# Second division of a window moved from unit 9 to unit 12, another choice of units whose second exponential goes to SBUF, and one store one place later in the queue

## The chip, the cores and the metric

The kernel runs on one core of a Trainium2 chip. The metric is the device time of one execution in microseconds (us). The kernel before was run three times: median 2611.41 us, from 2608.67 to 2623.45. Another execution was taken with the profiler; its rows are the ones shown below.

## The reference, cut to what matters

A cross-attention (64 pairs of batch and head, 1024 queries each from `x`; 1024 keys from `x` and 77 from `ctx_1024`, padded to 9 tiles of 128; head width 64), then a shared expert and a top-2 mixture of 8 experts. The part that the change touches is the softmax and its normalisation:

```python
sim = jnp.einsum('bhid,bhjd->bhij', qn, kn)
attn = jax.nn.softmax(sim, axis=-1)
out = jnp.einsum('bhij,bhjd->bhid', attn, v)
```

The kernel computes the unnormalised sum over the keys with the exponentials, gets the sum of the exponentials as a 65th row of the same product (V has a column of ones), and divides afterwards.

## The kernel before, in words

**Windows and units.** The attention runs in 32 windows of two heads (`WINDOWS`), preceded by two opening ones that only prepare. One window has 18 units (`UNITS`, 9 tiles of keys for each of two blocks g of 512 queries; both heads are in a unit, one in each half of the columns). So "the sums h = 0" (`o_sb[0]`, named o_first) are the first block of 512 queries of both heads, ready after unit 8, and h = 1 (`o_second`) those of the second block, ready after unit 17.

**One unit d** takes these steps. TensorE computes scores into one of two PSUM buffers, `ps_s[:, d % 2]` (line 975, 128 keys by 1024 columns). ScalarE takes the exponential twice: once rounded to fp32r as `pr_hi` (line 831), once in fp32 (line 832), either back into the same PSUM buffer or, for the units in `SPARED` (line 83, through `full_of`), into an SBUF buffer `pr[:, d % 2]`. VectorE subtracts the two to get the low part `pr_lo` (line 721); I call it the subtraction of unit d. TensorE multiplies V with both parts (line 1011, in two halves of the keys; line 997 for the first two units) into `ps_o`, two and three units later (`first`, `second`).

**What SPARED decides.** TensorE may write the scores of unit d + 2 into the buffer of unit d when nobody reads it any more: for a spared unit when the exponentials are done (`s_exp`), for the others when VectorE's subtraction is done (`s_lo`):

```python
wait(pe, s_exp if (d - 2) % UNITS in SPARED else s_lo, w.n(UNITS, d - 1))
```

The units after 17 are units 0, 1, ... of the next window. ScalarE waits before a spared unit for the subtraction two units before, because of the buffer `pr`.

**The sums.** After the ninth tile of keys VectorE copies the 65 x 1024 sums from PSUM to `o_sb[h]` (`output`, line 652): h = 0 ahead of the subtraction of unit 10, h = 1 ahead of that of unit 1 of the next window. `ps_o` is single, so TensorE's first product of the next block (unit 9, issued in `first` of unit 11; unit 0, in unit 2) waits for that copy through `s_o`.

**The division** is a round trip through DRAM. SyncE's queue stores the row of sums of exponentials and loads it back spread over 128 partitions (`spread`), VectorE inverts it (`invert`, line 681, after units 5 and 13), SyncE stores it and loads it broadcast to 64 partitions into `rec` (`broadcast`), and VectorE multiplies (`divide`, line 686): in the next window h = 0 after unit 7, h = 1 after unit 9. `rec` is one buffer for both. The result is stored by SyncE (`store`, line 322).

**Order on SyncE's queue in a window** (written out by hand, each entry with its waits): load the mask, spread h = 1, store h = 0, broadcast h = 1, load the weights `w_raw`, store h = 1, spread h = 0, broadcast h = 0, load `lnT_sb`. So the broadcast of h = 1 stands behind the store that waits for the division of h = 0 (unit 7).

**Other work in a window.** TensorE projects the next window's q, k and v tile by tile (lines 928 and 941) in units 6, 8, 11, 13 and 15 and transposes normalised tiles (line 905) in units 2, 4 and 6; ScalarE evacuates them (`raw`, line 776); GpSimd squares them (line 461), takes a power (line 463) and normalises (line 465). The last window but one has no projection, the last has no transposes either; the last also takes `lower(d)` steps for the stage that follows.

Of the kernel before, what the change touches and what calls it, by code (L numbers as in the profile page):

```python
# [79 lines left out]
HALVED = (8, 13, 15)  # L80
BETWEEN = 11
WHOLE = 2
SPARED = (0, 1, 9, 16, 17)
JOBS = TURNS + KT
PREP = [(c, g) for g in range(2) for c in range(C)] + [(c, None) for c in range(C)]
PREPS = len(PREP)
# [70 lines left out]
def attention(nc, carry, Wout, x, ctx_in, mask, ln_x_g, ln_x_b, ln_l_g, ln_l_b, qn_g, kn_g, lnT, Wq, Wkv, maskRow, maskCol, attT, rden, routed, out, Wfc_s, Wfc, w1S, o_second):  # L157

    with ExitStack() as ctx:
# [100 lines left out]
        def ring(w, d):  # L260

            return (2 * w.s + d) % RING

        def full_of(d):

            return pr[:, d % 2, :] if d in SPARED else ps_s[:, d % 2, :]

        def closing(w):

            return isinstance(w.v, int) and w.v == WINDOWS // 2 - 1  # L270
# [10 lines left out]
        def _(sp):  # L281
# [12 lines left out]
            def load_mask(b, slot):  # L294
                sp.dma_start(mrow[0:1, slot, :].bitcast(F32), maskRow[bass.ds(b, 1), :]).then_inc(s_mask[slot], 16)
                sp.dma_start(mcol[:, slot:slot + 1], maskCol[:, bass.ds(b, 1)], allow_slow_non_contiguous=True).then_inc(s_mask[slot], 16)

            def wait_then(sem, value):
                wait(sp, sem, value)
                sp.sem_inc(s_turn, 1)  # L300

            def spread(w, g, before):

                half = w.n(2, g - 2 * before)
                wait_then(s_o, w.n(2, g + 1 - 2 * before))
                sp.dma_start(rden[bass.ds(half, 1)].unsqueeze(0), o_sb[g][DH:DH + 1, :].unsqueeze(1)).then_inc(s_put, 16)
                wait_then(s_put, w.n(64, 32 * g + 16 - 64 * before))
                sp.dma_start(den[:, g, :], rden[bass.ds(half, 1)].rearrange("h (p k) -> p (h k)", p=P)).then_inc(s_den, 16)
# [11 lines left out]
            def store(w, g, before):  # L320
                wait_then(s_norm, w.n(2, g - 2 * before + 1))
                sp.dma_start(pair_v[g][bass.ds(w.n(1, -before), 1)].rearrange("w d r n -> d (w r) n"),
                             o_sb[g][0:DH, :].rearrange("d (r n) -> d r n", r=2)).then_inc(s_store[g], 16)
# [3 lines left out]
            def load_x(b):  # L327
                for h in range(2):
                    sp.dma_start(half_of(b, h).rearrange("p (t d) -> p t d", d=D), x_v[b][:, 4 * h:4 * h + 4, :]).then_inc(p_x[b % 2], 16)

            def keep(b):
                sp.wait_ge(p_split, 2 * PREPS * (b + 1))
                for part in range(2):
                    for c in range(C):
                        sp.dma_start(lnT[b][:, part, c], prepared(b, part, c).bitcast(F32)).then_inc(p_lnT if b else p_first, 16)
# [14 lines left out]
            def window(w):  # L350
                opening = isinstance(w.v, int) and w.v == -1
                mask_b, ln_b, pair = w.n(1, 1) // PAIRS, w.n(1, 3) // PAIRS, w.n(1, 3) % PAIRS
                if opening and w.s == 0:
                    sp.wait_ge(p_tp, PREPS + 4)
                    load_x(3)
                    keep(1)
                    sp.wait_ge(p_out, 32)
                if opening and w.s == 1:
                    keep(2)
                if closing(w) and w.s == 1:  # L360
                    for h in range(2):
                        sp.wait_ge(s_store[h], 16 * PAIRS)
                    carry.load_a(sp, attT, 0, 0, c_a0)
                if w.turn:
                    wait_then(s_exp, w.n(UNITS))
                    load_mask(mask_b, w.other)
                if w.attend and not w.first:
                    spread(w, 1, 1)
                    store(w, 0, 1)
                    broadcast(w, 1, 1)  # L370
                if w.proj and not (opening and w.s == 0):
                    wait_then(s_wlo, w.n(1, 3))
                    load_w(pair)
                if w.first:
                    sp.wait_ge(p_lnT, 192)
                if w.attend:
                    if not w.first:
                        store(w, 1, 1)
                    spread(w, 0, 0)
                    broadcast(w, 0, 0)  # L380
                    if closing(w) and w.s == 1:
                        store(w, 0, 0)
                if closing(w) and w.s == 0:
                    sp.wait_ge(s_v, w.n(2, 4))
                    sp.wait_ge(s_nrm, w.n(GROUPS, 2 * GROUPS))
                    for h in range(2):
                        k = slice(HH * h, HH * h + HH)
                        sp.dma_start(carry.wo[:, k, :], Wout.rearrange("(h k p) n -> h p k n", h=2, p=P)[h]).then_inc(c_wo, 16)
                if closing(w) and w.s == 1:
                    sp.wait_ge(c_lo, 2)  # L390
                    carry.load_a(sp, attT, 0, 1, c_a1)
                if opening and w.s == 0:
                    sp.wait_ge(p_first, 64)
                if opening and w.s == 1:
                    keep(3)
                if w.proj:
                    wait_then(s_raw, w.n(KT, 3 * KT))
                    if not (isinstance(w.v, int) and 2 * w.v + w.s == WINDOWS - 3):
                        load_ln(ln_b)
# [139 lines left out]
        def _(dve):  # L539
# [143 lines left out]
            def divide(w, h, before):  # L683

                dve.wait_ge(s_rec, w.n(32, 16 * h + 16 - 32 * before))
                v.tensor_tensor(o_sb[h][0:DH, :], o_sb[h][0:DH, :], rec[0:DH, :], ALU.mult).then_inc(s_norm, 1)
# [21 lines left out]
            def dve_windows(general):  # L708
                def window(w):
                    for d in range(UNITS):  # L710
                        if w.first and d == 0:
                            dve.wait_ge(p_lnT, 128)
                        if w.attend:
                            if general and d % KT == 0:
                                maximum(w, d // KT)
                            if d == 1 and not w.first:
                                output(w, 1, 1)
                            if d == KT + 1:
                                output(w, 0, 0)
                            dve.wait_ge(s_exp, w.n(UNITS, d + 1))  # L720
                            v.tensor_tensor(pr_lo[:, ring(w, d), :], full_of(d), pr_hi[:, ring(w, d), :].bitcast(F32),  # L721
                                            ALU.subtract).then_inc(s_lo, 1)
                        if w.attend and not w.first:
                            if d == 5:
                                invert(w, 1, 1)
                            if d in (7, 9):
                                divide(w, (d - 7) // 2, 1)
                        if w.attend and d == 13:
                            invert(w, 0, 0)
                        if closing(w) and w.s == 1 and d == 16:  # L730
                            divide(w, 0, 0)
                        if w.turn:
                            for i in TURNED.get(d, ()):
                                turned(w, i)
                        if w.turn and d in (3, 5):
                            values(w, d == 5)
                        if w.proj and d in (14, 17):
                            squares(w, (d - 14) // 3)
                        if closing(w) and w.s == 1 and d in (4, 6, 9, 11):
                            lower(d)  # L740
                        if d == 2 and not (isinstance(w.v, int) and (w.v == -1 or 2 * w.v + w.s == WINDOWS - 1)):
                            squares(w, 2 - GROUPS)
                        if isinstance(w.v, int) and w.v == -1:
                            opening(w, d)

                windows(dve, window)
                after = Window(WINDOWS // 2, 0)
                output(after, 1, 1)
# [4 lines left out]
        def _(act):  # L753
# [61 lines left out]
            def window(w):  # L815
                for d in range(UNITS):
# [4 lines left out]
                    if w.attend:  # L821
                        act.wait_ge(s_scores, w.n(UNITS, d + 1))
                        if d in SPARED:
                            wait(act, s_lo, w.n(UNITS, d - 1))
# [33 lines left out]
        def _(pe):  # L858
# [156 lines left out]
            def pe_windows(general):  # L1015
                def window(w):
# [21 lines left out]
                    def fresh(d):  # L1038
                        if w.attend:
# [4 lines left out]
                            if general and d % KT == 0:  # L1044
                                maximum(w, d // KT)
                            wait(pe, s_exp if (d - 2) % UNITS in SPARED else s_lo, w.n(UNITS, d - 1))
                            scores(w, d, general)
# [878 lines left out]
```

## Time and profile before

| what | value |
|---|---|
| median of three runs | 2611.41 us (2608.67 to 2623.45) |
| the profiled execution's own time | 2611.24 us |
| its span | 2609.4 us |
| around the span | 1.8 us |
| attention windows, first copy of sums h = 1 to last | 153.3 to 1786.3 us |
| TensorE matmul busy, VectorE, ScalarE, GpSimd | 2445.7, 1817.0, 1695.8, 1190.8 us |
| mean granted TensorE clock | 0.98 of full speed |

Time stamps are us from the start of the span. A row of a timeline has the start, the time until the end (of all of the instructions, where it ends with x2 or more), engine, line, operation, what it writes and reads, and in brackets how long the engine had been idle before and what ended that. Matmuls of one row are pipelined, so the next row starts before the last has ended.

### The profile page before, as it was taken

Reading aid. Unit: us, or ns where it says so; the run is one execution under the profiler, and the core shown is the slowest. Engines: PE = TensorE matmul, PEld = TensorE weight load, DVE = VectorE, ACT = ScalarE, POOL = GpSimd, SP = SyncE. Lnnn points to the kernel's source line nnn. Section 1 sums busy time; section 2 is a strip of 40 time slices with the busy share of each in tenths; the row PEclk is TensorE's granted clock in tenths of the full one; section 3 lists DMA queues with packets and bytes.
Section 4 is the critical chain, followed back from the end, with each engine's and each line's share of the span. In section 5 each row is a group of like instructions: output and inputs, shape, how many; then the busy total and the mean of one; then the engine's idle time right before and its main releaser. Section 6 shows DMA issues by size and latency. Waiting matters only on the chain. (4 is left out here: it accounts for less than half of the span.)

```text
span 2609.4 us, 53706 instructions
## 1 busy us (share of the span) xinstructions
PE 2445.7 (94%) x19926; PEld 1999.6 (77%) x19926; DVE 1817.0 (70%) x2452; ACT 1695.8 (65%) x2286; POOL 1190.8 (46%) x783
## 2 busy tenths in 40 slices
PE   4899999999999999999999999986989999999997
PEld 3677777777777777677767767655989999999997
DVE  7667766776677666776677667765876566777775
ACT  2678787887788778877887778873333334444443
POOL 4334433453344334443344334422533526666676
PEclk8899999999999999999999999998989999999999
DMA  6323232323332323223233323145731459999996
GB/s 195 138 80 110 95 98 79 121 80 98 92 114 82 100 88 110 86 96 100 86 111 95 88 86 113 46 119 121 171 94 67 147 166 320 321 321 317 323 322 172
DMA packets 231533, 363.26 MB, mean 139 GB/s; under 512 B 59559, under 2 KB 139739, under 8 KB 227400
## 3 DMA queue, kind: packets, MB, share of 16 engines
q1 hardware_dynamic: 204694, 301.66, 37.7%
q0 software_dynamic: 25696, 58.82, 7.8%
q8 instruction: 133, 2.18, 0.3%
q10 hardware_dynamic: 978, 0.34, 0.1%
q14 instruction: 32, 0.26, 0.0%
HBM read 280.90 MB, written 79.85 MB: 138 GB/s over the span
## 5 line engine op out<-in xcount | busy, mean ns | idle before, releaser
L831 ACT ACTIVATE pr_hi<-ps_s 128x1024 fp32r<-128x1024 f32 x512 | 527.3, 1030 | 246.7 <-PE ps_s L975 186.5
L721 DVE TENSOR_TENSOR pr_lo<-ps_s,pr_hi 128x1024 fp32r<-128x1024 f32 x416 | 504.2, 1218 | 240.7 <-ACT ps_s L832 240.7
L1011 PE MATMUL ps_o<-pr_hi,vA 64*65 64x512 f32 x2036 | 437.3, 399 | 64.9 <-DVE o_first L652 48.9
L463 POOL TENSOR_TENSOR rs<-ss,minus_half 128x16 f32<-128x16 f32 (+1 forms) x96 | 225.6, 2350 | 488.6 <-DVE ss L696 488.6
L1011 PE MATMUL ps_o<-pr_lo,vA 64*65 64x512 f32 x2036 | 430.8, 392 | 0.0
L1011 PE MATMUL ps_o<-pr_hi,vC 64*65 64x512 f32 x2036 | 430.0, 391 | 0.0
L1685 ACT ACTIVATE ht<-f_ps_h,b 128x256 f32<-128x256 f32 x440 | 184.4, 471 | 340.1 <-PE f_ps_h L1617 282.1
L721 DVE TENSOR_TENSOR pr_lo<-pr,pr_hi 128x1024 fp32r<-128x1024 f32 x160 | 288.2, 1816 | 159.5 <-ACT pr L832 154.8
L832 ACT ACTIVATE ps_s<-ps_s 128x1024 f32<-128x1024 f32 x384 | 395.4, 1030 | 0.0
L461 POOL TENSOR_TENSOR sq<-raw 128x1024 f32<-128x1024 f32 (+1 forms) x96 | 165.8, 1727 | 429.5 <-ACT raw L776 429.5
L1617 PE MATMUL f_ps_h<-xT_hi,w 128*128 128x256 f32 x1760 | 355.2, 285 | 2.8 <-DVE xT_lo L1719 2.3
L1630 PE MATMUL f_ps_y<-w,h_hi 128*128 128x256 f32 x1760 | 325.7, 283 | 0.0
L1617 PEld LDWEIGHTS f_ps_h<-xT_hi,w 128*128 128x128 f32 x1760 | 288.1, 190 | 3.5 <-DVE xT_lo L1719 2.9
L1544 POOL TENSOR_TENSOR w<-w2raw,w 128x1024 fp32r<-128x1024 f32 x80 | 213.4, 2668 | 169.7 <-ACT w L1671 169.7
L1011 PEld LDWEIGHTS ps_o<-pr_hi,vA 64*65 64x65 f32 x2036 | 160.8, 132 | 147.0 <-issue 71.7
L1630 PEld LDWEIGHTS f_ps_y<-w,h_hi 128*128 128x128 f32 x1760 | 272.3, 190 | 0.0
L975 PE MATMUL ps_s<-q_hi,k_hi 64*128 64x512 f32 x1152 | 246.8, 410 | 7.9 <-ACT pr L832 2.9
L1630 PE MATMUL f_ps_y<-w,h_lo 128*128 128x256 f32 x880 | 248.9, 283 | 0.0
L1617 PE MATMUL f_ps_h<-xT_lo,w 128*128 128x256 f32 x880 | 248.9, 283 | 0.0
L941 PE MATMUL ps_m<-w_sb,lnT_sb 64*128 64x384 f32 (+1 forms) x2304 | 242.7, 329 | 3.6 <-DVE k_lo L661 2.5
L975 PE MATMUL ps_s<-q_hi,k_lo 64*128 64x512 f32 x1152 | 237.4, 391 | 0.0
L975 PE MATMUL ps_s<-q_lo,k_hi 64*128 64x512 f32 x1152 | 237.3, 392 | 0.0
(220 smaller groups left out, 4676.2 us busy)
## 6 DMA issues: line engine op xcount, KB each, us to landing
w<-w1S_dram SPq DMA_DIRECT2D x160, 512.0 KB, 6.9
lnT_sb<-lnT_dram SPq DMA_DIRECT2D x31, 2304.0 KB, 9.0
w2raw<-in_L_ffn_Wproj SPq DMA_DIRECT2D x78, 512.0 KB, 7.1
w1S_dram<-cut POOLq DMA_DIRECT2D x36, 512.0 KB, 3.0
rec<-rden_dram SPq DMA_DIRECT2D x63, 256.0 KB, 3.7
routed_dram<-empty POOLq DMA_DIRECT2D x28, 387.0 KB, 3.6
xt<-routed_dram SPq DMA_DIRECT2D x39, 258.0 KB
w_raw<-in_L_xattn_Wkv SPq DMA_DIRECT2D x66, 128.0 KB, 2.9
```

Of the source, the lines that this page charges most:

```text
L461: g.tensor_tensor(sq[:, 0:n_, j0 * DH:], qk, qk, ALU.mult).then_inc(s_sq, 1)
L463: g.tensor_tensor(rs[:, 0:sums], ss[:, 0:sums], minus_half[:, 0:sums], ALU.pow).then_inc(s_pool, 1)
L721: v.tensor_tensor(pr_lo[:, ring(w, d), :], full_of(d), pr_hi[:, ring(w, d), :].bitcast(F32), ALU.subtract).then_inc(s_lo, 1)
L831: act.activation(pr_hi[:, ring(w, d), :], ps_s[:, d % 2, :], ACT.Exp, bias=bias)
L832: act.activation(full_of(d), ps_s[:, d % 2, :], ACT.Exp, bias=bias).then_inc(s_exp, 1)
L941: ins = mm(ps_m[:, tile % 2, lo:3 * PW], lnT_sb[rows, a, c, tile * P:(tile + 1) * P], w_sb[rows, w.slot, b, c, lo:], start=part == 0 and k ...
L975: ins = mm(ps_s[:, d % 2, 512 * h:512 * h + 512], key[rows, w.slot, keys], x[rows, w.slot, cols], start=not general and i == 0, stop=i == 2)
L1011: ins = mm(ps_o[0:DH + 1, h, :], v_[rows, h], p_[rows, 512 * h:512 * h + 512], start=k == 0 and part == 0 and i == 0, stop=k == KT - 1 and ...
L1544: nc.gpsimd.tensor_tensor(w2[:, slot, 2 * h:2 * h + 2, 1], w2raw[:, slot, 2 * h:2 * h + 2], w2[:, slot, 2 * h:2 * h + 2, 0].bitcast(F32), ...
L1617: ins = mm(ps_h[:, p % 2, i, :], w1[:, slot, p, k, lo, i, :], x_[:, parity, k, :], start=k_ == 0, stop=k_ == 3 * C - 1)
L1630: ins = mm(ps_y[:, parity, r, 0:D], h[:, parity, c, r * P:(r + 1) * P], w2[:, slot, p, lo, c % 2, :], start=c == 0 and k_ == 0, stop=c == ...
L1685: ins = act.activation(ht[:, p, i, :], ps_h[:, p % 2, i, :], ACT.Gelu_apprx_tanh, bias=b1[:, slot, p, i:i + 1])
```

## The change

The tuple `SPARED` loses units 16 and 17 and gains unit 10. So ScalarE's second exponential of units 16 and 17 goes back to PSUM and VectorE subtracts from there; that of unit 10 goes to `pr` in SBUF. By the wait quoted above, TensorE's scores of units 0 and 1 of the next window now wait for the subtractions of units 16 and 17, and those of unit 12 only for the exponentials of unit 10. `divide` of h = 1 moves on VectorE's queue from behind unit 9 to behind unit 12; in between lie the copy of the sums h = 0 and the subtractions of units 10 to 12. On SyncE's queue `spread` of h = 0 goes ahead of `store` of h = 1. Nothing is computed otherwise, and no instruction is added or removed.

```diff
-SPARED = (0, 1, 9, 16, 17)
+SPARED = (0, 1, 9, 10)
...
                 if w.attend:
+                    spread(w, 0, 0)
                     if not w.first:
                         store(w, 1, 1)
-                    spread(w, 0, 0)
                     broadcast(w, 0, 0)
...
                             if d == 5:
                                 invert(w, 1, 1)
-                            if d in (7, 9):
-                                divide(w, (d - 7) // 2, 1)
+                            if d in (7, 12):
+                                divide(w, (d - 7) // 5, 1)
                         if w.attend and d == 13:
                             invert(w, 0, 0)
```

## Rows read from the trace of the kernel before

**Rows 1.** The page, busy time, share of the span and instructions of TensorE
```profile
PE 2445.7 (94%) x19926; PEld 1999.6 (77%) x19926; DVE 1817.0 (70%) x2452; ACT 1695.8 (65%) x2286; POOL 1190.8 (46%) x783
```
**Rows 2.** Waits of TensorE: who waited <- for whom: total us, times, longest us
```profile
PE ps_o L1011 <- DVE o_first L652: 48.9, 31, 8.9
...
PE ps_o L1011 <- DVE pr_lo L721: 16.0, 30, 0.6
```
**Rows 3.** Waits of VectorE, the same columns
```profile
DVE o_second L686 <- DMA rec<-rden_dram: 86.0, 31, 8.6
```
**Rows 4.** Timeline of VectorE, units 9 to 13 of one window
```profile
864.15 1.22 DVE L686 TENSOR_TENSOR o_second<-o_second,rec 64x1024 f32<-64x1024 f32 x1 [2.34 <-DMA rec<-rden_dram]
865.29 1.21 DVE L652 COPY o_first<-ps_o 65x1024 f32<-65x1024 f32 x1
866.43 2.33 DVE L721 TENSOR_TENSOR pr_lo<-ps_s,pr_hi 128x1024 fp32r<-128x1024 f32 x2
870.66 1.22 DVE L721 TENSOR_TENSOR pr_lo<-ps_s,pr_hi 128x1024 fp32r<-128x1024 f32 x1 [1.90 <-ACT ps_s L832]
872.76 1.22 DVE L721 TENSOR_TENSOR pr_lo<-ps_s,pr_hi 128x1024 fp32r<-128x1024 f32 x1 [0.87 <-ACT ps_s L832]
```
**Rows 5.** Timeline of TensorE, the same window, units 11 and 12
```profile
862.73 0.46 PE L1011 MATMUL ps_o<-pr_hi,vC 64*65 64x512 f32 x2
862.96 0.47 PE L1011 MATMUL ps_o<-pr_lo,vA 64*65 64x512 f32 x2
863.36 2.37 PE L928 MATMUL ps_m<-w_sb,lnT_sb 128*128 128x384 f32 x12
866.65 0.45 PE L1011 MATMUL ps_o<-pr_hi,vA 64*65 64x512 f32 x2 [0.92 <-DVE o_first L652]
...
867.15 0.41 PE L1011 MATMUL ps_o<-pr_lo,vA 64*65 64x512 f32 x2
867.69 0.50 PE L975 MATMUL ps_s<-q_hi,k_hi 64*128 64x512 f32 x2
```
**Rows 6.** Timeline of GpSimd, its squares in two places
```profile
831.94 2.87 POOL L461 TENSOR_TENSOR sq<-raw 128x1024 f32<-128x1024 f32 x1
...
865.39 1.88 POOL L461 TENSOR_TENSOR sq<-raw 128x1024 f32<-128x1024 f32 x1 [14.31 <-ACT raw L776]
```
**Rows 7.** Timeline of VectorE, the subtractions of units 16 and 17
```profile
830.38 5.51 DVE L721 TENSOR_TENSOR pr_lo<-pr,pr_hi 128x1024 fp32r<-128x1024 f32 x2 [2.24 <-ACT pr L832]
```
**Rows 8.** Timeline of TensorE, scores of units 0 and 1, product of unit 17
```profile
831.63 0.43 PE L975 MATMUL ps_s<-q_hi,k_hi 64*128 64x512 f32 x2
...
833.86 0.40 PE L975 MATMUL ps_s<-q_hi,k_hi 64*128 64x512 f32 x2
...
835.02 0.40 PE L1011 MATMUL ps_o<-pr_lo,vA 64*65 64x512 f32 x2
835.95 0.45 PE L1011 MATMUL ps_o<-pr_hi,vA 64*65 64x512 f32 x2 [0.53 <-DVE pr_lo L721]
```
**Rows 9.** The subtraction's line by form: duration min/median/max in ns, first and last start
```profile
L721 DVE TENSOR_TENSOR pr_lo<-ps_s,pr_hi x416: 1203/1223/1226, 103.2 to 1778.8; 128x1024 fp32r<-128x1024 f32 x139
L721 DVE TENSOR_TENSOR pr_lo<-pr,pr_hi x160: 1208/1226/2912, 100.9 to 1783.3; 128x1024 fp32r<-128x1024 f32 x160
```
**Rows 10.** Timeline of ScalarE, the second exponential of unit 17
```profile
831.49 1.11 ACT L832 ACTIVATE pr<-ps_s,mcol 128x1024 f32<-128x1024 f32 x1
```
**Rows 11.** Timeline of TensorE, the three longest waits for the copy of the sums
```profile
1502.16 0.69 PE L1011 MATMUL ps_o<-pr_hi,vA 64*65 64x512 f32 x2 [3.91 <-DVE o_first L652]
...
1718.34 0.69 PE L1011 MATMUL ps_o<-pr_hi,vA 64*65 64x512 f32 x2 [8.90 <-DVE o_first L652]
...
1767.24 0.69 PE L1011 MATMUL ps_o<-pr_hi,vA 64*65 64x512 f32 x2 [6.03 <-DVE o_first L652]
```
**Rows 12.** Stretches: length, busy us of PE, PEld, DVE, ACT, POOL; PEclk; DMA share; GB/s
```profile
1506.00:1508.00 2.00, 2.00 (x12) 1.49 (x10) 1.01 (x1) 0.96 (x2) 0.00 (x0) 0.50 0.00 0
1508.00:1510.00 2.00, 2.00 (x22) 1.77 (x22) 0.21 (x1) 1.47 (x2) 0.00 (x0) 1.00 0.00 0
```

## The prediction

> **What bounds the kernel now.** I read the page's busy times first: TensorE is busy 94% of the span, every other engine 70% or less [rows 1]. So only what makes TensorE idle, or what lengthens its own work, can move the time. Next its waits [rows 2]: in the attention windows two of them repeat. 31 times (48.9 us in all, longest 8.9) the first product of a block waits for VectorE's copy of the sums h = 0, and 30 times (16.0 us, longest 0.6) a product waits for a subtraction. VectorE's own waits say why the copy is late: 31 times, 86.0 us in all, it stands at the division of h = 1 until `rec` has landed [rows 3]. The timelines show it in one window [rows 4, 5]: VectorE idles 2.34 us, divides at 864.15, and only then copies at 865.29; TensorE has finished the projection of unit 11 at 863.36 + 2.37 = 865.73 and waits 0.92 us for the copy, until 866.65. The copy itself could have begun when the ninth tile's products were done. The last of them start at 862.96; they are spaced by 0.23 us, and a copy that waits for nothing else starts some 0.3 us after that, by my estimate from their duration of 0.47: about 863.5. (Stamps below are those of this old window, unshifted.)
>
> **The change, part by part.**
>
> *The division behind unit 12.* The copy then runs from 863.5 to about 864.7, a full microsecond ahead of 865.73, so the wait goes. Over all windows 48.9 us are listed, of which 3.91, 8.90 and 6.03 belong to three long ones [rows 11]; the other 28 give 48.9 - 18.8 = 30.1 us, 1.07 us each. All of it should go: **30.1 us**.
>
> What else the late copy cost: the scores of unit 12 wait for the subtraction of unit 10, which stands behind the copy, at 866.43 [rows 4]. TensorE's starts are 0.54 apart there (867.15 to 867.69) where its pitch is 0.23 [rows 5], so 0.31 us, in 28 windows **8.7 us**. With unit 10 spared these scores need only the exponentials.
>
> The three long waits come from a `rec` that landed late (longest wait of VectorE 8.6 us). The divisions now come at least 6 us later in the queue, so nearly all of this is absorbed. In the last two windows TensorE has no projection in unit 11 to cover the copy, and in the last one another step of VectorE stands between; I leave 1.5 us of wait in each, so 18.8 - 3.0 = 15.8 us go. Behind each long wait the granted clock is at 0.50, the lower of its two levels (1.2 GHz), which TensorE had reached while it idled: in the first case from 1502.16 until about 1508 [rows 11, 12], 5.8 us at half speed, so 2.9 us lost. The matmul of 0.69 us instead of 0.45 shows the same behind the other two. I take 2 us each for these (an estimate from the first). With waits of 1.5 us or less that goes too: 6.9 us. Together **22.7 us**.
>
> The division itself, 1.22 us, comes behind the subtraction of unit 12, which ends at 871.9; that of unit 13 starts at 872.76. So 0.87 us of it lies in idle time [rows 4], and the subtraction of unit 13 is up to 0.4 us later. TensorE needs that for the scores of unit 15, with the projection of two tiles between: covered, cost 0. If that cover were gone it would cost 0.4 us a window, 12 us. `rec` had landed at 864.15, 7.7 us ahead.
>
> *Unit 10 from SBUF.* The subtraction takes 1208 to 2912 ns from SBUF, 1226 in the median, against 1203 to 1226 from PSUM [rows 9]. It would start at about 864.7, and GpSimd's squares begin at 865.39 [rows 6]. At 1.2 us it ends at 865.9, that of unit 11 at 867.1; TensorE wants the latter for the scores of unit 13, which fall 9 groups of 0.23 after those of unit 12 (866.4), at 868.5. So even 1.3 us more costs nothing; I take 0, with 0 to 1.3 us a window as bounds.
>
> *Units 16 and 17 from PSUM.* Now these two subtractions take 5.51 us together [rows 7], while GpSimd normalises and squares; the product of unit 17 waits for the second (starts 0.93 apart instead of 0.23, so 0.70 us) [rows 8]. From PSUM they take 1.23 each, and none of 416 took over 1226 ns [rows 9], many of them beside GpSimd. That frees 30 x 0.70 = 21 us. Against it stands the new wait: the scores of units 0 and 1 need them. Unit 16: VectorE starts at 830.38, ends at 831.6, TensorE wants it at 831.63: nothing to 0.1. Unit 17: its exponential ends at 831.49 + 1.11 = 832.60 [rows 10], the subtraction at 833.85; TensorE came to those scores at 833.86, and would come 0.14 us sooner at its pitch: 0.1 to 0.2. Together I take 0.2 us (0 to 0.7), so 30 x 0.5 = **15 us**. ScalarE no longer waits for the buffer either, which only makes these units earlier.
>
> The trace shows no difference between the sources when GpSimd is quiet. The Trainium skill ("VectorE: DVE Perf Modes", the section on the TRN2 errata) instead gives a PSUM source 62 cycles more than an SBUF one; by that, an estimate from the page, the two chained subtractions would add 0.13 us a window, 4 us of the gain. The medians of 1223 and 1226 ns speak against it here.
>
> *SyncE's queue.* Spread h = 0 in front of store h = 1 is needed, since that store now waits for unit 12, and the copy's row is there before. The store's 0.7 us of issue then precedes the broadcast of h = 0, which is wanted only in unit 7 of the next window: cost 0. Only in the last window it is wanted in unit 16, with about 1 us to spare: 0 to 2 us once, I take 0.5.
>
> **Sum**: 30.1 + 8.7 + 22.7 + 15 - 0.5 = 76 us. The profiled execution took 2611.24 us, 0.2 us from the median of the runs, so the same holds for both: 2611.2 - 76 = **2535 us**. A measurement of this kernel tells about 0.5% (13 us) from no change.
>
> **The rivals.**
>
> *A. The squares get ahead of unit 10* (6%). At its GpSimd collisions a subtraction from SBUF took 2.75 us on average [rows 7], and GpSimd's squares 2.87 instead of 1.88 [rows 6]. If the squares start before the subtraction of unit 10, it ends when they do plus 1.2: 865.39 + 1.88 + 1.2 = 868.5, unit 11 at 869.7, and the scores of unit 13 are 1.2 us late; in 30 windows 36 us: 2571 us. For it: the two are only 0.7 us apart. Against it: the squares need a tile whose projection TensorE starts after the products that the copy waits for, then an evacuation. The Trainium skill ("SBUF — State Buffer", section Who interferes with whom) says that of a VectorE instruction with two SBUF inputs and a GpSimd one that reads SBUF, the later blocks until the first is done. By that the order alone decides this rival; the 5.51 us agree with it.
>
> *B. The window's end turns into a bound* (8%). Exponentials, subtraction and scores are a closed chain over two units, in which TensorE has nothing else to do in units 16 to 1. If VectorE comes to these subtractions 0.7 us later than I think in each window, say behind its squares of unit 15, the 15 us are gone and 6 more are lost: 2556 us. Against it: VectorE idled 2.24 us ahead of unit 16 [rows 7].
>
> *C. Slower than before* (2%). The same place, the scores of units 0 and 1. The rest of the change gives 61 us, or 2 us a window; so the kernel gets slower only if the two new waits cost over 2 us more than the 0.7 removed, say 3.4 us: 30 x 3.4 = 102, 2611 - 61 + 102 - 21 = 2631 us. That needs both subtractions from PSUM to take 2.9 us, as the worst from SBUF do, and a further late step. The 416 of rows 9 speak against it.
>
> *D. It does not do what it says* (2%): `rec` lands late at unit 12 as well and TensorE waits in unit 15 instead. With 7.7 us to spare that needs every window to be like the worst. No change, 2611 us.
>
> **How the numbers follow.** The forecast has 82%. The low end adds what I left out: no new waits (6 us), and the small start-up gaps behind each wait (0.2 us in each of 60 cases, 12 us): 2517. The high end reaches over B, 2556. Faster by over 0.5%: forecast, A, B, 0.96; the same 0.02; slower 0.02.
>
> **What would show it.** In the profile after: no wait of TensorE for the copy of o_first except some 1.5 us in each of the last two windows; VectorE's wait at the division of h = 1 near zero; windows of 50.3 us in the mean instead of 52.7 ((1786.3 - 153.3) / 31, less 76 / 31); subtractions from PSUM x448 at 1.22 us and 128 from SBUF with a mean near 1.25 (unit 10 is the test of A); a clock of 1.00 in the stretch about 1500. I am wrong if the scores of unit 13, 0 or 1 show a repeated wait for the subtraction of over 0.3 us, if ScalarE's exponentials become what TensorE waits for, or if the gain is under 50 us.

## The result and the profile after

The changed kernel takes 2516.4 us in the median (2515.45 to 2516.98, four runs), the kernel before, beside it, 2612.98 us. The ratio is 0.9624, 95% interval 0.9595 to 0.9653. The forecast was 2535 us with a range of 2517 to 2556: the direction and the places were right, the gain of 76 us was too small, and the time lies 0.6 us below the low end. The profiled execution took 2515.45 us (span 2513.9), 95.8 us less than that of before.

The page of the changed kernel, busy time by engine, answering to [rows 1]:

```profile
PE 2414.2 (96%) x19926; PEld 1996.5 (79%) x19926; DVE 1714.7 (68%) x2452; ACT 1699.3 (68%) x2286; POOL 1190.7 (47%) x783
```

TensorE's waits in the changed kernel (total us, times, longest), the row that answers to the first of [rows 2]:

```profile
PE ps_o L1011 <- DVE o_first L652: 5.5, 2, 4.0
```

31 waits of 48.9 us have become 2 of 5.5 together, and the 30 waits for a subtraction (16.0 us) are no longer in the list. In VectorE's waits the 86.0 us at the division [rows 3] are gone too; a short new one has come, which matters below (VectorE's waits of the changed kernel, the same columns):

```profile
DVE o_first L652 <- DMA attT_dram<-o_first: 4.5, 1, 4.5
```

The subtraction's line by form (count, minimum, median and maximum duration in ns), as in [rows 9]:

```profile
L721 DVE TENSOR_TENSOR pr_lo<-ps_s,pr_hi x448: 1207/1224/1227, 103.4 to 1691.1; 128x1024 fp32r<-128x1024 f32 x150
L721 DVE TENSOR_TENSOR pr_lo<-pr,pr_hi x128: 1209/1220/1240, 101.1 to 1676.4; 128x1024 fp32r<-128x1024 f32 x128
```

The longest subtraction from SBUF is now 1240 ns where it was 2912. One regular window, VectorE's timeline of units 9 to 13, answering to [rows 4]:

```profile
876.27 1.23 DVE L721 TENSOR_TENSOR pr_lo<-pr,pr_hi 128x1024 fp32r<-128x1024 f32 x1 [2.80 <-ACT pr L832]
879.20 1.22 DVE L652 COPY o_first<-ps_o 65x1024 f32<-65x1024 f32 x1 [1.71 <-PE ps_o L1011]
880.34 1.21 DVE L721 TENSOR_TENSOR pr_lo<-pr,pr_hi 128x1024 fp32r<-128x1024 f32 x1
881.47 1.21 DVE L721 TENSOR_TENSOR pr_lo<-ps_s,pr_hi 128x1024 fp32r<-128x1024 f32 x1
884.93 1.23 DVE L721 TENSOR_TENSOR pr_lo<-ps_s,pr_hi 128x1024 fp32r<-128x1024 f32 x1 [2.24 <-ACT ps_s L832]
886.07 1.21 DVE L686 TENSOR_TENSOR o_second<-o_second,rec 64x1024 f32<-64x1024 f32 x1
887.20 1.21 DVE L721 TENSOR_TENSOR pr_lo<-ps_s,pr_hi 128x1024 fp32r<-128x1024 f32 x1
```

The copy now waits for TensorE's products and for nothing else, starts at 879.20, and the division waits for nothing. TensorE in the same window, answering to [rows 5]:

```profile
878.68 0.42 PE L1011 MATMUL ps_o<-pr_lo,vA 64*65 64x512 f32 x2
879.02 2.35 PE L928 MATMUL ps_m<-w_sb,lnT_sb 128*128 128x384 f32 x12
881.31 0.44 PE L1011 MATMUL ps_o<-pr_hi,vA 64*65 64x512 f32 x2
881.59 0.39 PE L1011 MATMUL ps_o<-pr_hi,vC 64*65 64x512 f32 x2
881.82 0.39 PE L1011 MATMUL ps_o<-pr_lo,vA 64*65 64x512 f32 x2
882.05 0.39 PE L975 MATMUL ps_s<-q_hi,k_hi 64*128 64x512 f32 x2
```

No bracket stands behind the projection, and the scores of unit 12 follow at the pitch of 0.23.

**Where the 95 us came from.** From the timelines I took, for each window, the time between the starts of the first score products of neighbouring units (line 975), and averaged it over windows 1 to 29 (counted from 0), those that project. A window begins with its unit 0; the one that starts at 831.63 in [rows 8] is window 14. Windows of even and odd number differ before the change, so they stand apart; why they differ no run here shows. The steps that are not shown differ by less than 0.05 us between the two kernels. In us:

| kernel, windows | 3 to 4 | 5 to 6 | 6 to 7 | 11 to 12 | 12 to 13 | 17 to 0 | 0 to 1 | 1 to 2 | window |
|---|---|---|---|---|---|---|---|---|---|
| before, even | 4.88 | 2.10 | 3.70 | 6.16 | 2.31 | 2.09 | 2.23 | 2.83 | 53.00 |
| before, odd | 4.58 | 2.28 | 3.94 | 6.05 | 2.17 | 2.09 | 2.20 | 2.83 | 52.77 |
| after, even | 4.63 | 2.08 | 3.60 | 4.57 | 2.08 | 2.17 | 2.15 | 2.17 | 50.11 |
| after, odd | 4.59 | 2.06 | 3.64 | 4.54 | 2.06 | 2.20 | 2.17 | 2.18 | 50.11 |

By the copies of o_second: windows 1 to 29 went from 1533.6 to 1453.2 us (80.4), the last two from 99.4 to 88.0 (11.3), what is behind them from 823.1 to 819.8 (3.3; in all kernels of this study it lies between 817.1 and 823.1, without any order that I can see), and what is ahead by 0.4.

The steps 11 to 12 and 1 to 2 fell as foreseen. The surprise is in steps 3 to 4, 5 to 6 and 6 to 7, where the change touches nothing: before, an even window lost 0.37 us there (most of it in step 3 to 4) and an odd one 0.52 us (in steps 5 to 6 and 6 to 7), 13 us in 29 windows. (Two of my expectations below speak of 0.5 us in units 5 to 7 and of 0.75 us in the slower windows; the 0.75 comes from counting step 3 to 4 of an even window together with the later steps of the odd one ahead of it.)

### The profile page after: what moved, and what is told of

Its sections match the earlier page's. It is cut to its first block and busy times, and to the rows that moved or that the text cites. A ratio compares the mean times of both kernels' runs of the same rounds, so it can differ in the third digit from the quotient of the medians.

```text
span 2513.9 us, 53674 instructions
## 1 busy us (share of the span) xinstructions
PE 2414.2 (96%) x19926; PEld 1996.5 (79%) x19926; DVE 1714.7 (68%) x2452; ACT 1699.3 (68%) x2286; POOL 1190.7 (47%) x783
## 3 DMA queue, kind: packets, MB, share of 16 engines
q8 instruction: 133, 2.18, 0.3%
## 5 line engine op out<-in xcount | busy, mean ns | idle before, releaser
L721 DVE TENSOR_TENSOR pr_lo<-ps_s,pr_hi 128x1024 fp32r<-128x1024 f32 x448 | 546.6, 1220 | 312.7 <-ACT ps_s L832 312.5
L1011 PE MATMUL ps_o<-pr_hi,vA 64*65 64x512 f32 x2036 | 432.0, 394 | 5.5 <-DVE o_first L652 5.5
L461 POOL TENSOR_TENSOR sq<-raw 128x1024 f32<-128x1024 f32 (+1 forms) x96 | 145.0, 1510 | 430.4 <-ACT raw L776 430.4
L1544 POOL TENSOR_TENSOR w<-w2raw,w 128x1024 fp32r<-128x1024 f32 x80 | 206.2, 2578 | 175.9 <-ACT w L1671 175.9
L941 PEld LDWEIGHTS ps_m<-w_sb,lnT_sb 64*128 64x128 f32 x2304 | 214.6, 186 | 23.2 <-DVE k_lo L661 2.9
L1723 DVE CAST h_hi<-ht 128x512 fp32r<-128x512 f32 x220 | 114.7, 521 | 173.3 <-ACT ht L1685 162.5
```

What stands on the lines that cost most here:

```text
L461: g.tensor_tensor(sq[:, 0:n_, j0 * DH:], qk, qk, ALU.mult).then_inc(s_sq, 1)
L941: ins = mm(ps_m[:, tile % 2, lo:3 * PW], lnT_sb[rows, a, c, tile * P:(tile + 1) * P], w_sb[rows, w.slot, b, c, lo:], start=part == 0 and k ...
L1011: ins = mm(ps_o[0:DH + 1, h, :], v_[rows, h], p_[rows, 512 * h:512 * h + 512], start=k == 0 and part == 0 and i == 0, stop=k == KT - 1 and ...
L1544: nc.gpsimd.tensor_tensor(w2[:, slot, 2 * h:2 * h + 2, 1], w2raw[:, slot, 2 * h:2 * h + 2], w2[:, slot, 2 * h:2 * h + 2, 0].bitcast(F32), ...
```

## The experiments

**First group: the parts of the change by themselves.** What is the loss in units 3 to 7, and what is unit 10 worth?

Only the division and the queue:

```diff
-SPARED = (0, 1, 9, 10)
+SPARED = (0, 1, 9, 16, 17)
```

> Only the division of h = 1 moved behind unit 12, and the spread ahead of the store; SPARED as before (0, 1, 9, 16, 17). My theory: the change has two parts that add up, the late copy of the sums (unit 11, late rec) and VectorE's subtractions from SBUF at the window's end, which cost TensorE at the scores of unit 2 and, by VectorE's backlog, in units 5 to 7. Then here the step from the scores of unit 11 to those of 12 falls from 5.92 to about 4.56 us, the steps 5 to 6, 6 to 7 and 1 to 2 stay at 2.27, 3.92 and 2.83, a window takes 51.2 us, and the kernel about 2557 us. Rival: the 0.5 us of units 5 to 7 come from the division's move (SyncE's and VectorE's order in the first half of the window); then those steps fall to 2.07 and 3.62, a window takes 50.7 us and the kernel about 2542.

Measured: 2548.3 us (2546.41 to 2548.88; ratio 0.9754, 0.9733 to 0.9776). Step 11 to 12 fell to 4.55 and 4.58; the steps stayed at 4.89 (3 to 4, even windows), 2.29 and 3.94 (5 to 6 and 6 to 7, odd windows), and 1 to 2 at 2.84. So my theory holds and the rival falls. A window takes the 51.2 us I expected, and yet the time is 9 us under my 2557. I take most of that to come from my having set out from the median window of before, where windows with a very late `rec` make the mean longer.

Only `SPARED = (0, 1, 9, 10)`, the division behind unit 9:

> Only SPARED = (0, 1, 9, 10); the division of h = 1 stays behind unit 9. My theory: steps 5 to 6, 6 to 7 and 1 to 2 fall to 2.07, 3.62 and 2.17 us, the step 11 to 12 falls only by the 0.3 to 0.4 us of the scores that no longer wait for the subtraction of unit 10, so to about 5.5; a window takes 51.2 us, the kernel about 2568. Rival: steps 5 to 7 stay as before, then 51.7 us and 2582.

Measured: 2571.4 us (2562.77 to 2576.98; ratio 0.9834, 0.9805 to 0.9863). Steps 3 to 4, 5 to 6, 6 to 7 and 1 to 2 are 4.61, 2.07, 3.64 and 2.16, as in the changed kernel; step 11 to 12 is 6.24 in even and 5.89 in odd windows. Three of the 29 windows have a step of over 9 us there; the others have 5.7 in the mean, where I expected 5.5. Only units 16 and 17:

> Only units 16 and 17 taken out of SPARED (0, 1, 9). My theory: as with SPARED = (0, 1, 9, 10), but the step 11 to 12 stays at 5.9: a window 51.6 us, the kernel about 2580. The rival for units 5 to 7 (they owe nothing to units 16 and 17): 52.1 us and 2594.

Measured: 2581.8 us (2571.86 to 2586.66; ratio 0.9879, 0.9842 to 0.9915), the same steps at 4.62, 2.06, 3.63 and 2.16. So what units 3 to 7 lost belongs to the subtractions of units 16 and 17 of the window before.

How it gets there can be read in the kernel before, VectorE from unit 16 of window 14 on (window 15 starts at 884.21):

```profile
882.89 5.52 DVE L721 TENSOR_TENSOR pr_lo<-pr,pr_hi 128x1024 fp32r<-128x1024 f32 x2 [2.23 <-ACT pr L832]
...
896.04 0.29 DVE L694 TENSOR_REDUCE ss<-sq 128x2 f32<-128x128 f32 x1 [0.42 <-POOL sq L461]
...
898.86 1.22 DVE L721 TENSOR_TENSOR pr_lo<-ps_s,pr_hi 128x1024 fp32r<-128x1024 f32 x1
...
906.95 1.23 DVE L721 TENSOR_TENSOR pr_lo<-ps_s,pr_hi 128x1024 fp32r<-128x1024 f32 x1 [1.82 <-ACT ps_s L832]
```

Apart from the 0.42 us in which it waits for GpSimd's squares, which are late themselves, VectorE has no idle time for 22 us, until 905.1. The subtraction at 898.86 is that of unit 4; it ends at 900.08, and TensorE starts the scores of unit 6 at 900.13, 0.44 us after its last product instead of 0.23. In the changed kernel VectorE has room: at each copy of the sums h = 1 it now waits for TensorE, which before it did once (VectorE's waits, after and then before):

```profile
DVE o_second L652 <- PE ps_o L1011: 35.2, 31, 1.9
...
DVE o_second L652 <- PE ps_o L1011: 1.7, 1, 1.7
```

The changed kernel with unit 10 back in PSUM:

> The changed kernel with SPARED = (0, 1, 9), so unit 10 is subtracted from PSUM again. My theory: unit 10's place is worth nothing once the copy is early, since its subtraction ends half a microsecond before the scores of unit 12 are due: 2516 us, step 11 to 12 still 4.56. Rival: it is worth the 0.3 to 0.4 us a window that the old trace showed at these scores: step 11 to 12 at 4.9, 2527 us.

Measured: 2516.6 us (2515.94 to 2519.49; ratio 0.9639), step 11 to 12 at 4.55: unit 10's place in `SPARED` is worth nothing here. With the late copy it was worth some 5 us in windows 1 to 29 (1506.1 - 1501.0 in the two kernels above, from one profiled execution each, whose runs spread by more than that).

In windows 1 to 29 the parts are additive within 2 us: the division's part gives 1533.6 - 1483.9 = 49.7 us and `SPARED` on top of it 1483.9 - 1453.2 = 30.7; `SPARED` alone gives 1533.6 - 1501.0 = 32.6. The division's part has the new place of `spread` in it; no run has that alone on the kernel before.

**Second group: queue, place of the division, and the new wait.**

SyncE's old order in the changed kernel:

```diff
                 if w.attend:
-                    spread(w, 0, 0)
                     if not w.first:
                         store(w, 1, 1)
+                    spread(w, 0, 0)
```

> The changed kernel with SyncE's old order: store of h = 1 ahead of spread of h = 0. My theory: the spread then waits for the division behind unit 12, the row is inverted some 3 us later and VectorE waits for it at the reciprocal behind unit 13, but it has 2.7 us of idle time there and the subtraction of unit 14 is not due: under 0.3 us a window, 2516 to 2524 us. Rival: the swap is what lets the rest work; the wait of VectorE reaches TensorE at the scores of unit 15 or 16 with 1 us or more a window, 2546 us or more.

Measured: 2542.4 us (2540.89 to 2544.23; ratio 0.974, 0.9717 to 0.9762). I had priced this order at nothing to 8 us; it costs 26, so my theory is wrong here and the rival's 2546 us is near, though its place is not. VectorE's waits in this kernel have a new row:

```profile
DVE den L681 <- DMA den<-rden_dram: 128.0, 31, 5.9
```

and VectorE's timeline of one window of it, units 13 to 17:

```profile
950.19 0.20 DVE L681 RECIPROCAL den<-den 128x8 f32<-128x8 f32 x1 [4.46 <-DMA den<-rden_dram]
950.31 1.20 DVE L721 TENSOR_TENSOR pr_lo<-ps_s,pr_hi 128x1024 fp32r<-128x1024 f32 x1
951.42 1.21 DVE L694 TENSOR_REDUCE ss<-sq 128x16 f32<-128x1024 f32 x1
...
959.72 1.22 DVE L694 TENSOR_REDUCE ss<-sq 128x16 f32<-128x1024 f32 x1 [1.32 <-POOL sq L461]
```

The wait at the reciprocal is indeed longer than the idle time there. It makes VectorE's reduction of the squares late, GpSimd's power, normalisation and next squares follow from it, VectorE waits for those (1.32 us), and enters the crowded first units of the next window late. Step 3 to 4 is back at 4.87 in even windows, steps 5 to 6 and 6 to 7 at 2.19 and 3.91 in odd ones, although the subtractions of 16 and 17 come from PSUM, and VectorE's waits for TensorE at the copy of the sums h = 1 are down to 4 of 3.5 us together. No engine but VectorE has a new wait for a transfer in these windows, so the loss comes by way of VectorE: **whatever made VectorE late at the window's end, most of the price was paid by TensorE in units 3 to 7**, some 11 of the 1467.8 - 1453.2 = 14.6 us of windows 1 to 29. The last two windows cost 11.4 us more (99.4 against 88.0), with one wait of TensorE of 4.79 us for a subtraction behind this reciprocal.

The division behind unit 10:

```diff
-                            if d in (7, 12):
-                                divide(w, (d - 7) // 5, 1)
+                            if d in (7, 10):
+                                divide(w, (d - 7) // 3, 1)
```

> The changed kernel with the division of h = 1 behind unit 10 instead of 12. My theory: only its place behind the copy counts. rec has landed some 1 us before in most windows, the division delays the subtraction of unit 11 by 1.1 us, which ends just as the scores of unit 13 are due: 0 to 0.3 us a window, 2516 to 2524 us. Rival: the distance to unit 12 is needed because rec is late; then the step 12 to 13 grows by 1 us and the kernel takes 2545 us.

Measured: 2562.4 us (2559.93 to 2563.91; ratio 0.9814, 0.979 to 0.9837), step 12 to 13 at 3.52 instead of 2.07. That is 46 us over the changed kernel: my 0 to 0.3 us a window is refuted, and the rival's 1 us is exceeded, but not for its reason: `rec` was there in all windows but one, where VectorE waited 1.3 us. VectorE's timeline of one window of this kernel, units 10 to 12:

```profile
953.80 1.21 DVE L721 TENSOR_TENSOR pr_lo<-pr,pr_hi 128x1024 fp32r<-128x1024 f32 x1
954.93 2.91 DVE L686 TENSOR_TENSOR o_second<-o_second,rec 64x1024 f32<-64x1024 f32 x1
957.77 2.34 DVE L721 TENSOR_TENSOR pr_lo<-ps_s,pr_hi 128x1024 fp32r<-128x1024 f32 x2
```

GpSimd's timeline at the same place:

```profile
954.51 2.25 POOL L461 TENSOR_TENSOR sq<-raw 128x1024 f32<-128x1024 f32 x1 [14.28 <-ACT raw L776]
```

and TensorE's, the scores of unit 13:

```profile
959.03 0.50 PE L975 MATMUL ps_s<-q_hi,k_hi 64*128 64x512 f32 x2 [1.26 <-DVE pr_lo L721]
```

The squares begin at 954.51, get going when unit 10's subtraction ends at 955.0, and end at 956.76; the division reads two SBUF operands, begins at 954.93 and ends at 957.84, 1.1 us after the squares. It waited them out. 29 of the 31 divisions took that long. This is the mechanism of my rival A (the squares get ahead of a VectorE instruction with two SBUF inputs, and the scores of unit 13 are late), with the division in the place of unit 10's subtraction. The Trainium skill ("SBUF — State Buffer", section Who interferes with whom) says that the later of the two is blocked until the first is done; the rows agree.

Unit 11 spared as well, to make its subtraction meet the squares:

> The changed kernel with unit 11 spared as well, so its subtraction reads two SBUF buffers just as GpSimd starts its squares. A test of the rule that the later of the two waits for all of the other: the squares have been waiting since unit 10's subtraction, run first, and the subtraction of unit 11 takes about 3 us instead of 1.21, the squares 2.3 as now. If the two share the port instead, both take some 1.5 times as long. Either way TensorE waits for the exponentials only and the time stays at 2516 to 2519 us.

Measured: 2516.6 us (2515.88 to 2517.53; ratio 0.9638). The time is as expected, the rows are not: I expected 3 us for the subtraction of unit 11. VectorE's timeline of this kernel, the subtractions of units 10 and 11:

```profile
930.82 2.35 DVE L721 TENSOR_TENSOR pr_lo<-pr,pr_hi 128x1024 fp32r<-128x1024 f32 x2
```

GpSimd's squares there:

```profile
931.54 3.38 POOL L461 TENSOR_TENSOR sq<-raw 128x1024 f32<-128x1024 f32 x1 [14.28 <-ACT raw L776]
```

Both subtractions ran back to back and undisturbed, and the squares waited for both (3.38 us instead of 1.88, and much the same in all windows that project). They had been waiting since 931.54, so the order of arrival alone does not decide. In the kernel ahead, with the same distance, the squares got in between. So at a handover between two VectorE instructions either can win; what decides it these runs don't show. The two kernels together exclude that the engines share at 1.5 times the duration each.

GpSimd held back at the start of its work for the last window:

```diff
             def window(w):
                 if not isinstance(w.v, int):
                     clear(w)
+                if closing(w) and w.s == 1:
+                    pool.wait_ge(s_o, w.n(2, -1))
                 if w.attend:
                     split1(w.v, w.v + 1, w.s)
```

> The changed kernel with GpSimd held back at the start of its work for the last window until the sums h = 0 of the last window but one are copied, so that its 512 KB weight transfers do not run beside the store of h = 0. My theory: in the last window but one the copy waits 4.46 us for that store (7.5 us to landing instead of 3.2); then it lands in about 3.2 us, TensorE's wait of 3.97 us falls to about 1.5 and the kernel takes 2513 to 2515 us. Rival: the store is late for another reason, or the transfers then delay the last window by as much: 2516 to 2518 us.

Measured: 2511.0 us (2510.72 to 2512.09; ratio 0.9618, 0.9596 to 0.964): 5.4 us less than the changed kernel, twice what I expected, and the fastest kernel of this study. Window 30 in the changed kernel, VectorE's timeline:

```profile
1630.80 1.22 DVE L652 COPY o_first<-ps_o 65x1024 f32<-65x1024 f32 x1 [4.46 <-DMA attT_dram<-o_first]
```

and a stretch of it, with the columns of [rows 12]:

```profile
1630.00:1635.00 5.00, 2.83 (x14) 2.17 (x16) 3.49 (x3) 0.00 (x0) 3.61 (x3) 0.66 0.20 55
```

TensorE's wait for that copy:

```profile
1632.16 0.69 PE L1011 MATMUL ps_o<-pr_hi,vA 64*65 64x512 f32 x2 [3.97 <-DVE o_first L652]
```

With GpSimd held back, VectorE's timeline at the same copy:

```profile
1627.94 1.22 DVE L654 COPY o_first<-ps_o 65x1024 f32<-65x1024 f32 x1 [1.96 <-PE ps_o L1013]
```

TensorE's wait:

```profile
1629.30 0.45 PE L1013 MATMUL ps_o<-pr_hi,vA 64*65 64x512 f32 x2 [1.47 <-DVE o_first L654]
```

and the same stretch:

```profile
1630.00:1635.00 5.00, 5.00 (x46) 3.85 (x45) 3.51 (x4) 3.89 (x4) 3.22 (x4) 1.00 0.23 88
```

`o_sb[0]` may not be overwritten before its store has landed. Beside GpSimd's transfers of 512 KB that store took 7.5 us, without them 3.1. (In the kernel before it took 7.55 us in this window too, but the late copy did not need it.) The window shrinks from 47.4 to 43.2 us: 2.5 us of TensorE's wait, and some 1.7 us by the clock, whose mean in that stretch of 5 us is 1.00 instead of 0.66. I had priced the wait and forgotten the clock behind it.

**Third group: the cause at the window's end, and unit 11.**

The kernel before with two steps of GpSimd cut short (its normalisation of tiles 0 to 3 and its squares of tiles 4 to 7):

```diff
+                if less and k == 1:
+                    g.tensor_tensor(sq[:, 0:1, 0:DH], raw[:, first:first + 1, 0:DH], raw[:, first:first + 1, 0:DH], ALU.mult).then_inc(s_sq, 1)
...
+                if less and k == 0:
+                    g.tensor_tensor(nrm[:, 0:1, 0:1, :], raw[:, 0:1, 0:DH].rearrange("p t (j d) -> p t j d", d=DH),
...
```

> The kernel before, with GpSimd's normalisation of the first four tiles and its squares of the next four cut to one column block of 64 in every window but the opening ones (the output is not the reference's; the rest of the work is there). Units 16 and 17 are still subtracted from SBUF. My theory: those subtractions are slow only because they meet these two steps of GpSimd, and TensorE's loss in units 1 to 2 and 3 to 7 comes from that. So they take at most 1.24 us, the step 1 to 2 falls from 2.83 to about 2.2, the steps 3 to 7 of the slower windows lose their 0.75 us, a window takes about 51.7 us and the kernel 2578 us. Rival: subtracting from SBUF is what costs, with or without GpSimd; then the steps stay and so does the time, 2605 us or more.

Measured: 2573.2 us (2570.61 to 2574.06; ratio 0.9848, 0.9823 to 0.9872). The 160 subtractions from SBUF have a mean of 1248 ns where it was 1816; the row of the groups by form (busy us, mean ns, idle before):

```profile
L730 DVE TENSOR_TENSOR pr_lo<-pr,pr_hi 128x1024 fp32r<-128x1024 f32 x160 | 199.6, 1248 | 188.8 <-ACT pr L841 184.2 <-issue 4.6
```

Step 1 to 2 is 2.08, step 3 to 4 is 4.62 in even windows (4.68 in odd ones, where it was 4.58), steps 5 to 6 and 6 to 7 are 2.06 and 3.63 in odd windows. Windows 1 to 29 take 1503.6 us, 30.0 less than before; the two kernels above with 16 and 17 out of `SPARED` and the late division gained 27.5 and 32.6 us there. So SBUF as a source costs nothing by itself here; meeting these two steps of GpSimd does. The subtraction of unit 17 takes 1.23 us in the mean where it took 2.91, that of unit 16 1.33 where it took 2.69, so my bound of 1.24 was not met by unit 16; one other took 2.31.

The division behind unit 11 (`d in (7, 11)`):

> The changed kernel with the division of h = 1 behind unit 11. Behind unit 10 it started while GpSimd's squares were under way, took 2.91 us and held up the subtraction of unit 11. My theory: behind unit 11 it still meets the end of the squares and takes some 1.9 us, but VectorE has 2.2 us of idle time there, so nothing is late: step 12 to 13 at 2.08, 2516 us. Rival: every position ahead of unit 12 costs, because the scores of unit 13 or 14 are near: the step 12 to 13 or 13 to 14 grows by 0.3 us or more, 2526 us.

Measured: 2516.2 us (2514.79 to 2516.26; ratio 0.9631). The row of the division in one window:

```profile
883.04 1.78 DVE L686 TENSOR_TENSOR o_second<-o_second,rec 64x1024 f32<-64x1024 f32 x1
```

It meets the end of the squares, takes 1.78 us, and nothing is late: step 12 to 13 is 2.07, as I expected. The number 12 itself is not needed; being behind the copy is, and not being caught by the squares ahead of unit 11's subtraction.

## Why the prediction was too low, point by point

**The division, its scores and the clock: right.** Predicted for windows 1 to 29: 30.1 + 8.7 + 3.9 + 2.9 = 45.6 us; measured with the division alone 49.7. The rest is in step 12 to 13, which fell by 0.11 us in the usual window, a startup behind the wait that I put at the low end only, and by 1.76 us in window 26, the one of the long wait. The copy starts 0.52 us after the last products before it, not 0.3, which changes nothing.

**Units 16 and 17 from PSUM: the step that failed, a term of half its size.** I took 0.70 - 0.2 = 0.5 us a window, 15 us in all, from the one wait that stood beside these units [rows 8]. Measured in windows 1 to 29: 30.7 us. At the place itself the gain is close to what I said (1 to 2: 0.66; 0 to 1: 0.03 to 0.08; 17 to 0: -0.11 to -0.08 for the new wait), some 18 us. The other 13 are the 0.37 us (even windows) and 0.52 us (odd ones) of units 3 to 7, which I put at nothing without asking. I asked what the 5.5 us of VectorE [rows 7] made late right behind them and stopped there; VectorE has almost no idle time from unit 16 to unit 6 of the next window, so it carried the lateness along, in part by way of GpSimd, into waits of TensorE that are too short to stand high in the list. How much of it GpSimd's own lateness adds no run separates. Moving the division alone left them untouched, taking 16 and 17 out of `SPARED` alone took them away, and the old queue brought them back by another lateness.

**Unit 10 from SBUF: right, and worth nothing.** It costs nothing and, with the copy early, gains nothing. The 8.7 us that I put beside it came from the early copy alone, so my sentence beside it, that with unit 10 spared these scores need only the exponentials, credits a part that was not needed. Rival A did not happen here; its mechanism came with the division behind unit 10, at 1.45 us a window where I had 1.2.

**SyncE's queue: right for the change, but the reason was thin.** I called the swap needed and did not price its absence; with the division behind unit 12 it is worth 26 us.

**The three long waits: one right, two too high.** Predicted for the last two windows 9.4 + 6.5 us, measured 5.5 + 5.8. In the last one TensorE's wait is 1.48 us as said. In the one before I missed the store that must land before its buffer is written again: 3.97 us of wait instead of 1.5, and a clock that is lower again behind it.

**Other stages**: nothing predicted, 3.7 us measured, within what these stages vary by.

The missed 13 us, the 4 of step 12 to 13 and the 3.7 elsewhere, less 4.6 in the last two windows, and 3 more at the window's end (17.7 against 14.5) make up the difference of 19. The range's low end allowed 18, for other reasons (no new waits, startups), so that the time comes so near it is luck: the 13 us of units 3 to 7 are not in it. The mean window takes 49.7 us, where I had 50.3 (by my own numbers 50.2).

**Two side questions of the prediction.** With one input in PSUM the subtraction has a median of 1224 ns, with both in SBUF 1220 ns (after). The Trainium skill ("VectorE: DVE Perf Modes", the section on the TRN2 errata) gives a PSUM source 62 cycles more than an SBUF one; the trace does not agree for this instruction. What did set the price of units 16 and 17, and of the division's place, is that the instruction and GpSimd's ran one after the other.

## What to carry to other kernels

When an instruction on a crowded engine is slow, its price is not the wait that stands next to it: follow the lateness along that engine until the first real idle time, and look at short waits that repeat there, in each kind of iteration apart. An instruction that waits for a round trip belongs behind the ones on which the bound engine depends, and every queue on the way has to be reordered with it; ask also which transfer must have landed before the work that has been made early may start. A VectorE instruction with two SBUF operands took 1.21 or 2.91 us here, by what GpSimd did in that microsecond.

## What the hardware showed unexpectedly

VectorE's instructions with two SBUF operands and GpSimd's squares of an SBUF tile excluded each other: 2.91 us for a division that takes 1.21 alone, 3.38 us for squares that take 1.88. Which of them gets in when a third instruction ends was different in two kernels with nearly the same distances. Of the 448 subtractions with one operand in PSUM none took over 1227 ns (after). In window 30 the granted clock was lower about the end of TensorE's wait of 3.97 us (mean 0.66 in the stretch shown), and 1.00 in the same stretch with a wait of 1.47 us in the held-back kernel.
